# Attention layer kernel: a step that works on eight batch elements in place of four

## The reference

```python
q = heads(x @ Wq + bq); k = heads(x @ Wk + bk); v = heads(x @ Wv + bv)
scores = einsum('bhqd,bhkd->bhqk', q, k) / sqrt(64)
probs  = softmax(scores + where(adj, 0, -9e15)[:, None], axis=-1)
ctx    = einsum('bhqk,bhkd->bhqd', probs, v)          # heads joined to 384
out    = layernorm(x + (ctx @ Wf + bf), axis=-1)      # eps 1e-5
```

## Time and profile before

| | before |
|---|---|
| median of 3 runs | 1001.26 us (1001.25 to 1001.6) |
| the profiled execution: its own time | 1002.12 us |
| its span in the trace | 1000.3 us |
| PE busy, PEld busy | 991.7 us (99%), 900.2 us |
| DVE, POOL, ACT busy | 706.7, 633.1, 589.5 us |
| DMA: mean rate over the span | 178 GB/s |
| granted PE clock | full in every slice (2.4 GHz) |

### The profile page before, as it was taken

One profiled execution on the slowest core, in us unless ns is written; L12 is line 12 of the kernel. 1 busy time (PEld: TensorE's weight loads), 2 busy tenths in 40 slices (PEclk: granted clock), 3 DMA queues, 4 the chain that ended last, 5 costly groups with the idle time before them and its releaser, 6 DMA issues.

```text
span 1000.3 us, 27877 instructions
## 1 busy us (share of the span) xinstructions
PE 991.7 (99%) x7690; PEld 900.2 (90%) x7690; DVE 706.7 (71%) x2760; ACT 589.5 (59%) x2130; POOL 633.1 (63%) x653
## 2 busy tenths in 40 slices
PE   9999999999999999999999999999999999999997
PEld 8788999889999889998899988999988999889997
DVE  5676766867668667677676686766777766867667
ACT  4766545675446665466654566554666545675556
POOL 2446657567566576575675765766656657567566
PEclk9999999999999999999999999999999999999999
DMA  8776676666776666766667666667666676665543
GB/s 186 175 196 167 172 210 189 178 163 171 199 193 186 168 170 175 218 172 182 161 176 204 188 178 169 173 183 207 181 173 168 171 215 181 176 171 160 160 151 104
DMA packets 344780, 178.08 MB, mean 178 GB/s; under 512 B 228784, under 2 KB 328752, under 8 KB 344752
## 3 DMA queue, kind: packets, MB, share of 16 engines
q1 hardware_dynamic: 343264, 176.77, 64.8%
q10 hardware_dynamic: 1488, 0.98, 0.3%
HBM read 103.35 MB, written 74.32 MB: 178 GB/s over the span
## 4 chain that ended last, share of the span: by engine, by line
PE 97%; ACT 1%; DVE 0%; DMA 0%; issue 0%; POOL 0%; SPq 0%; POOLq 0%; DVEq 0%
PE work_ps L427 16%; PE work_ps L429 15%; PE work_ps L428 15%; PE scores_ps L446 9%; PE scores_ps L466 9%; PE scores_ps L427 7%; PE scores_ps L429 7%; PE scores_ps L428 7%; PE work_ps L508 6%; PE scores_ps L508 6%; ACT probs L866 1%; DMA x_in<-in_x 0%; ACT qT L894 0%; PE scores_ps L545 0%; PE scores_ps L556 0%
## 5 line engine op out<-in xcount | busy, mean ns | idle before, releaser
L866 ACT ACTIVATE probs<-probs,neg_max 128x128 f32<-128x128 f32 x768 | 297.5, 392 | 87.9 <-DVE neg_max L676 87.9
L1038 POOL TENSOR_TENSOR probs<-probs,inv_sum 128x768 f32<-128x768 f32 x128 | 188.3, 1471 | 152.0 <-DVE inv_sum L699 152.0
L676 DVE CUSTOM_DVE_ANT_0 probs<-scores_ps,mask_bias 128x128 f32<-128x128 f32 x768 | 167.3, 286 | 127.9 <-PE scores_ps L446 127.2
L875 ACT COPY v_sb<-work_ps 128x384 f32<-128x384 f32 x128 | 61.3, 479 | 263.4 <-PE work_ps L429 263.4
L1033 POOL TENSOR_SCALAR y_sb<-y_sb,mean_var,rstd 128x384 f32<-128x384 f32 x120 | 198.4, 1653 | 21.5 <-POOL rstd L1023 21.5
L1023 POOL TENSOR_TENSOR rstd<-var_eps,minus_half 128x1 f32<-128x1 f32 x128 | 86.5, 676 | 168.5 <-DVE var_eps L720 168.5
L866 ACT ACTIVATION_READ_ACCUMULATOR probs<-probs,neg_max 128x1 f32 x768 | 146.9, 191 | 0.0
L1017 POOL TENSOR_TENSOR x_bias<-x_in,bias_row 128x384 f32<-128x384 f32 x128 | 128.9, 1008 | 7.7 <-DVE bias_row L829 7.7
L427 PE MATMUL scores_ps<-wf_hi,cT_hi 128*128 128x384 f32 x384 | 129.3, 337 | 0.0
L429 PE MATMUL scores_ps<-wf_hi,cT_lo 128*128 128x384 f32 x384 | 129.2, 336 | 0.0
L428 PE MATMUL scores_ps<-wf_lo,cT_hi 128*128 128x384 f32 x384 | 129.1, 336 | 0.0
(11 more groups left out here) (94 smaller groups left out, 2068.1 us busy)
## 6 DMA issues: line engine op xcount, KB each, us to landing
p_out<-p_turned SPq DMA_DIRECT2D x125, 384.0 KB, 2.8
pT<-p_out SPq DMA_DIRECT2D x500, 96.0 KB, 2.8
x_in<-in_x SPq DMA_DIRECT2D x128, 192.0 KB, 2.9
x_blocks<-in_x SPq DMA_DIRECT2D x372, 64.0 KB, 2.3
out<-y_sb SPq DMA_DIRECT2D x120, 192.0 KB, 2.1
adj_u<-in_adj SPq DMA_DIRECT2D x32, 64.0 KB, 2.1
out<-xT SPq DMA_DIRECT2D x4, 192.0 KB, 2.7
out<-qT SPq DMA_DIRECT2D x4, 192.0 KB, 1.9
```

Source lines behind the costliest of these rows:

```text
L676: last = nc.vector.tensor_tensor_reduce(out=probs[:, e, h, :], in0=scores_ps[:, score_cols(e, h)], in1=mask_bias[:, e, :], scale=-SCALE, s ...
L866: last = nc.scalar.activation(probs[:, e, h, :], probs[:, e, h, :], ACT.Exp, bias=neg_max[:, e, h:h + 1], scale=-1.0, accum_out=row_sum[:, ...
L1038: nc.gpsimd.tensor_tensor(probs[:, e, :, :], probs[:, e, :, :], inv_sum[:, e, :].unsqueeze(2).broadcast_to([P, HEADS, SEQ]), ALU.mult).the ...
```

## The change

A step now works on a set of eight elements (`SET`), 16 sets. PE's order in a step becomes: scores of elements 0 to 3, two Q/K jobs of the next set in row halves, scores of 4 to 7, two more halved jobs, contexts of all eight elements of the set before (in chunks of 128 features over four elements, 512 columns in a bank), the remaining eight Q/K jobs with the whole array, then results of four, V of four, results of four, V of four. The work per element is the same; per eight elements four Q/K jobs are in row halves, as before.

With it go: (a) V is evicted into `v_next` and a DMA of SP moves all eight elements' V (128 rows of 12,288 bytes, 1.57 MB) into `v_sb` once the contexts of the set before are done (`move_v`); (b) `x_in` has four slots, the bias is added in place, `x_blocks` is single, and their loads stand elsewhere in SP's order; (c) the contexts are rounded and split by chunks of 512 columns, three per four elements, and `out_product` waits for all three chunks of its half; (d) the first step takes the exponentials in half elements between the evictions of Q and K; (e) at the end one element is turned by PE in place of three. `p_turned` still has two buffers.

```diff
@@ PE @@
-            def step(i, c):
-                scores(i, c)
-                for j in range(HALVED):                 # HALVED = 2
-                    qk_halves(i, c + 1, j)
-                for e in range(GROUP):
-                    ctx_product(i, c - 1, e)
-                for j in range(HALVED, NJ):
-                    qk_product(i, c + 1, j)
-                for e in range(GROUP):
-                    out_product(e, n - GROUP + e)
-                for e in range(GROUP):
-                    v_product(i, c + 1, e)
...
+            def step(s):                                # HALVED = 4
+                if halved(s + 1):
+                    scores(s, 0)
+                    for j in (0, 1):
+                        qk_halves(s + 1, j)
+                scores(s, 1)
+                if halved(s + 1):
+                    for j in (2, 3):
+                        qk_halves(s + 1, j)
+                    for half in range(2):
+                        ctx_chunks(s - 1, half)
+                for j in range(HALVED if halved(s + 1) else 0, 2 * NJ):
+                    qk_product(s + 1, j)
+                for half in range(2):
+                    if not is_step(s, 0):
+                        for e in range(half * GROUP, (half + 1) * GROUP):
+                            out_product(s - 1, e)
+                    if half == 0 or not is_step(s, LAST - 1):
+                        for e in range(half * GROUP, (half + 1) * GROUP):
+                            v_product(s + 1, e)
...
-                pe.wait_ge(cT_split, n + 1)
+                pe.wait_ge(cT_split, ctx_count(s, half, KC - 1))
@@ SP @@
+            def move_v(s):
+                past(sp, v_copied, s * SET + SET - 1)
+                past(sp, ctx_done, s * 2 * KC - 1)
+                sp.dma_start(v_sb[:, :, :], v_next[:, :, :]).then_inc(v_moved, DMA)
...
+                if not is_step(s, 0):
+                    for e in (0, 1):
+                        store_blocks(s, e)
+                    move_v(s)
+                    load_blocks(s, 0)
+                    for e in (2, 3, 4):
+                        store_blocks(s, e)
+                        load_blocks(s, e - 1)
...
+                if more:
+                    load_x_blocks(s + 2, 1, range(0, 6))
+                for e in (5, 6):
+                    store_blocks(s, e)
+                    load_blocks(s, e - 1)
+                if more:
+                    load_x_blocks(s + 2, 1, range(6, 12))
+                store_blocks(s, 7)
+                for e in (6, 7):
+                    load_blocks(s, e)
@@ DVE @@
+                past(dve, p_stored[e % 2], s * GROUP + e // 2 - 1, per=DMA)   # in turn_blocks(s, e)
...
+                turn_blocks(s, 4)
+                invert_sums(s, 6)
+                turn_blocks(s, 5)
+                invert_sums(s, 7)
+                for m in range(2):
+                    turn_blocks(s, 6 + m)
+                    if not is_step(s, 0):
+                        split_ctx(s - 1, 0, m)
+                if not is_step(s, 0):
+                    split_ctx(s - 1, 0, 2)
```

More of the change, by code:

```diff
@@ L33 @@
 GROUP = 4
+SET = 2 * GROUP
 GTOK = GROUP * SEQ
-GROUPS = BATCH // GROUP
-LAST = GROUPS - 1
-TURN = 2
+SETS = BATCH // SET
+LAST = SETS - 1
 BANK = 512
@@ L73, in past, with run_steps, is_step @@
     eng.wait_ge(sem, value)
-def run_steps(eng, step, first=0, turns=TURNS):
-    for g in range(first, TURN):
-        step(g // TURN, g % TURN)
-    with eng.Fori(1, turns) as i:
-        for c in range(TURN):
-            step(i, c)
-    for g in range(turns * TURN, LAST):
-        step(g // TURN, g % TURN)
+def run_steps(eng, step):
+    for s in range(FIRST_LOOPED):
+        step(s)
+    with eng.Fori(FIRST_LOOPED, END_LOOPED) as i:
+        step(i)
+    for s in range(END_LOOPED, LAST):
+        step(s)
+def is_step(s, n):
+    return isinstance(s, int) and s == n
 def attention_block(nc, x, adj, wq, bq, wk, bk, wv, bv, wf, bf, out):
@@ new lines, in x_slot, with split_ctx_at @@
+        def x_slot(n, e):
+            if isinstance(n, int) and n >= BATCH - GROUP:
+                blocks = x_blocks[:, :, :, :].rearrange("p k t j -> p (k t j)")
+                return blocks[:, e % GROUP * HID:(e % GROUP + 1) * HID]
+            return x_in[:, e % GROUP, :]
+        def split_ctx_at(s, half):
+            if half and isinstance(s, int) and s >= LAST - 1:
+                at = s - LAST + 1
+                return xT_hi[:, at, :, :], xT_lo[:, at, :, :]
+            return cT_hi[:, :, :], cT_lo[:, :, :]
@@ L444, in scores @@
+            def scores(s, half):
+                pe.wait_ge(qk_copied, copies(s, (half + 1) * NJ - 1))
+                if halved(s) and half == 0:
+                    pe.wait_ge(qk_summed, sums(s, HALVED - 1))
+                for e in range(half * GROUP, (half + 1) * GROUP):
                     for h in range(HEADS):
+                        t = e % GROUP * MATS + h // 2
+                        if t % 4 == 0 and h % 2 == 0:
+                            wait_for_score_pair(s, half, t // 4)
@@ new lines, in ending @@
+            def ending():
+                scores(LAST, 0)
+                for e in range(GROUP, SET):
+                    v_product(LAST, e)
+                scores(LAST, 1)
+                for half in range(2):
+                    ctx_chunks(LAST - 1, half)
+                for e in range(SET):
+                    out_product(LAST - 1, e)
+                transpose_last_p()
+                ctx_chunks(LAST, 0)
+                last_contexts()
+                for e in range(SET):
+                    out_product(LAST, e)
@@ L923, in normalise_late @@
[L923 to L934 removed]
+                past(act, v_moved, s - 1, per=DMA)
@@ new lines, in copy_v, with copy_qk @@
+                nc.scalar.copy(v_next[:, e, :], v_bank(s, e)[:, 0:HID]).then_inc(v_copied, 1)
+            def copy_qk(s, j):
+                dst, col = job(j)
+                past(act, qk_done, s * 2 * NJ + j)
+                past(act, scores_done, (s - 1) * SET + j // NJ * GROUP + GROUP - 1)
+                if halved(s) and j < HALVED:
+                    nc.scalar.activation(dst, bank(HALF_PAIRS[j][0]), ACT.Identity, bias=col, scale=1.0
+                                         ).then_inc(half_copied, 1)
+                else:
+                    nc.scalar.activation(dst, qk_bank(s, j), ACT.Identity, bias=col, scale=1.0
+                                         ).then_inc(qk_copied, 1)
@@ new lines, in ending @@
+                for m in (1, 2):
+                    round_ctx(s - 1, 0, m)
+                for e in range(GROUP, SET):
+                    exps(s, e)
+                for n in BY_SCALAR[:3]:
+                    normalise_late(n)
+                copy_last_pT()
+                normalise_late(BY_SCALAR[3])
+                for half in range(2):
+                    for m in range(KC):
+                        round_ctx(s, half, m)
+                for n in BY_SCALAR[4:]:
+                    normalise_late(n)
@@ L1084, in _ @@
+                for e in range(SET):
+                    add_bias(s, e)
+                for e in range(6, SET):
+                    normalise_y(s - 1, e)
+                for e in range(SET):
+                    normalise_y(s, e)
             beginning()
```

1212 lines of the change are left out of this document (703 added, 509 removed).

## The result

The changed kernel takes 1304.63 us, the median of 4 runs (1302.98 to 1306.78); the kernel before takes 1001.37 us beside it. The ratio is 1.303, with a 95% interval of 1.301 to 1.304. The forecast was 1052, so slower was right, and the size, 51 us forecast and 303 measured, was far off. One execution of a kernel of experiment 6 (e7) took 2737.83 us, for a reason that nothing on record shows; it is left out of that kernel's time.

A forecast was written before the change was run, and what follows sets the result against it. PE's own work was taken as the bound (99% busy). 1002.1 less 9.3 and 1.5 gives 991.3; waits of 4.6 in 13 steps and 1.4 in step 14 add 61.2: 1052.5, forecast 1052 us, range 1018 to 1082.

The forecast's parts named there:

- The edges between shapes: PE's array-shape changes: 0.58 us a cycle, 16 cycles fewer, 9.3 us less; halved jobs to scores taken as costing nothing.
- The first step's 1.5 us: First step: PE's wait for an eviction behind whole-element exponentials goes with half elements, 1.5 us less.
- DVE starts on the masks at 1.9: Start of a step's chain: DVE begins the masks 1.9 us after the scores start, needing 1.3 per element.
- Four low parts of x at 0.48: DVE behind element 3's reciprocal: four operations at 0.48 us, done at 17.8, element 0 turned at 18.8.
- V's move: SP's 1.57 MB transfer just ahead of loads 0 and store 2: delays store 2, +2.4 at most with the slow store.
- the slow store: A store right behind another element's loads: its loads back begin 3.9 us later and not 2.8, +1.1.
- Three landings and SP's order: Chain through SP: store 2 lands at 26.3, store 5 at 36.5, DVE's two chunks are split at 38.7.
- PE waits 4.6 us, 14 times: Before the result products: 4.6 us (3.05 to 5.5) in steps 1 to 13, 1.4 in step 14; 61.2 in all.
- the least value of 3.05: Lower bound of PE's wait before the results: PE there at 35.65, DVE's splits done at 38.7.
- Waits at the end: The ending with one turned element: put at 0 with other small changes, from -1.5 to +2.5, the last for these waits.
- 1.9 and 5.3: DVE's start on the masks and its time for four elements' masks, summed in the chain to 7.0.
- The slow move: Rival: V's transfer at 182 GB/s holds up the store another 4.3 us, about 1108; chance 0.15 together with late x.

The follow-up runs named there:

- experiment 6: Kernels with all repairs to the changed kernel at once and SP's order varied, two of them with a reordered ending; 1161.75, 1058.70 and 1044.82 us.
- e7: Changed kernel with VectorE's loop moved, x splits first, context splits before turns 6 and 7, V's move behind element 5's loads and x_blocks behind it; 1161.75 us.
- e12: e7 with the ending reordered, and x 4 to 7 and two stores of y ahead of the x_blocks; V's move behind element 5's loads; 1044.82 us.
- e5: Changed kernel with 24 more instructions at the start of VectorE's program, moving its loop; 1231.92 us.
- e3: Changed kernel with VectorE's splits of x for elements 4 to 7 ahead of the reciprocals of elements 0 to 3; 1261.17 us.
- e4: Changed kernel with V's move cut to one of eight elements from step 1 on, only its time read; 1251.57 us.
- e14: e12 with the last contexts rounded ahead of ScalarE's normalisations and the last set's probabilities of three elements transposed on PE, not one; 1033.31 us.
- e6: Kernel before the change with 92 more instructions at the start of VectorE's program, moving its loop; 1030.14 us.

## Why the prediction was wrong, point by point

- **The edges between shapes: right.** The step at 171.33, where DVE does not pause, has scores in 2.70, halved jobs in 4.25, scores in 2.59, halved jobs in 4.28 and contexts in 5.39 us (5.4 forecast), with no gap from halved jobs to scores. A step without a wait (e12) takes 61.00 against 61.36; of the 0.58 a cycle 0.36 is seen in it.
- **The first step's 1.5 us: right.** Its Q/K jobs take 12.4 us against 14.3.
- **"DVE starts on the masks at 1.9": wrong by 3.1 and then 4.4 us a step, and it is the largest error.** The forecast took DVE's loop to run as in the kernel before. It weighed instructions by what they do and never by where they lie. Worth 72.7 us (e5). Nothing in the rows of before pointed to it except a loop that did not pause.
- **"Four low parts of x at 0.48": wrong by 4.8 us a step**, worth 43.5 us (e3). The price came from operations that ran with no GpSimd multiplication beside them; the chain put the four right behind the reciprocals that set GpSimd going. The place in the chain changed the price, and the forecast did not weigh what GpSimd would be doing beside them.
- **V's move: mechanism right, size short.** It stood in the way as described, but cost 3.8 us a step (e4), 4.9 with the slow store, outside the bounds of 0 and 2.4; the part missing was that SP itself stood, 5.0 us for four issues. Worth 53.1 us (e4).
- **Three landings and SP's order (12.4 us from store 2's landing to PE): right.** It measured 12.8.
- **"PE waits 4.6 us, 14 times": place and count right, size wrong** (12.6), as the sum of the above: the least value of 3.05, turn 0 later by 11.3 (6.6 from the pause, the rest from x), 4.9 on the way, less the 6.6 by which PE itself came later, 12.65. Step 14, where 1.4 was forecast, waited 9.8: the x_blocks that it lacks are worth 2.6 us and not 3.2, and all the rest came on top there too.
- **Missing: what the clock costs behind a wait.** 1.7 us of results at the lower clock in each step, and 2.1 in the halved jobs. The sum had no term for it.
- **"Waits at the end", up to 2.5 us: wrong**, 26.8. I had judged the ending by its count of instructions and not followed its chain.
- **A slip without effect.** 1.9 and 5.3 are 7.2 and not 7.0; the next four masks wait for PE's scores, so nothing hangs on it.
- **The rivals.** The slow move (1108) named the right transfer for a part; no case had a stall that no semaphore explains. None reached 1305, and the range did not allow for a chain whose prices all came from a quieter place. That the direction was right owes nothing to luck: the wait that was named is there. But two of its three large causes, the pause behind the branch and GpSimd beside the splits, were in no case of the forecast.

No version tried beats the kernel before: the best, e14, is 3.1% slower. Its steps 2 to 13 take 61.65 us in the mean (61.0 to 62.8) against 61.36, and its first and last sets cost more.

## What to carry to other kernels

Count the instructions of each engine's loop and of what stands ahead of it: a loop that just fails to fit the fetched blocks costs microseconds a pass (here 4 to 5), shows as "issue" idle time behind the branch and as instruction packets, and is moved by a few instructions. Price an operation by a row with the same neighbours, above all DVE beside GpSimd, and follow the chain of the ending as closely as that of a step. A chain that passes through one in-order queue can be repaired by order, without fewer bytes: here SP's order alone took the step from 69 us (e7) to 61 (e12).

## What the runs showed of the hardware

- Instruction packets of 8192 B, by their places one for some 128 instructions, ran five to a pass of a loop of 275 instructions that paused for 3.7 to 5.1 us at each branch back (two packets inside the pause); moved by 24 instructions it had none and paused for 0.22. A loop of 266 instructions that had no packets went from 0.27 to between 2.8 and 3.6 us once moved by 92. By the places of the packets and the count of instructions the slow loops touch four blocks of 128 instructions and the quick ones three. The Trainium skill, page "Runtime: NRT & Kernel Launch", section "Instruction fetch mechanics", says that a taken branch to a target outside the fetched window forces a fetch; the trace agrees and adds the price. The page has blocks of 16 KiB, two in a window. The runs speak for half of that: in e6 the packets start some 4, 20 and 134 instructions behind the branch and 5 ahead of it, near the block ends at 4, 132 and 260 that the count gives.
- DVE's fp32 subtraction of 128x384 with both inputs in SBUF took 0.48 us apiece with GpSimd idle, 1.74 beside GpSimd's multiplications.
- A transfer of 1.57 MB from SBUF to SBUF landed after 7.9 us, with other transfers beside it, and three of the four issues behind it took 1.9, 1.7 and 1.0 us in place of 0.45.
- Matmuls behind a wait of 12.5 us ran at half clock for 3.7 us, 0.32 apart in place of 0.17.
